# Order of transfers and of the key work in a three-part decoder kernel: the residual load goes ahead of the next x, and the preparation is rearranged

## The reference, cut to what matters

```
# 1. mixing: 8 heads of 64, fft along the head, running sum over the tokens
q, k, v = split(x @ w_qkv);  fq, fk, fv = fft(q), fft(k), fft(v)
kv = cumsum(fk * fv, over tokens)
x = layernorm(x + ifft(kv * conj(fq)).real @ w_out)
# 2. cross attention on the context: 16 heads of 32
q, k, v = x @ W_q + b_q, ctx @ W_k + b_k, ctx @ W_v + b_v
x = layernorm(x + softmax(mask(q k^T / sqrt(32))) v @ W_o + b_o)
# 3. feed-forward: kernel rounded to 4 bits, plus a low-rank term
scale = max(abs(kernel)) / 7;  w = clip(round(kernel / scale), -8, 7) * scale
x = layernorm(x + x @ w + bias + (x @ a) @ b)
```

## Time and profile before

| | us |
|---|---|
| median of 3 runs | 970.46 (970.12 to 971.36) |
| the profiled execution, its own time | 969.73 |
| its span | 967.9 |

### The profile page before, as it was taken

One profiled execution on the slowest core, in us unless ns is written; L12 is line 12 of the kernel. 1 busy time (PEld: TensorE's weight loads), 2 busy tenths in 40 slices (PEclk: granted clock), 3 DMA queues, 4 the chain that ended last, 5 costly groups with the idle time before them and its releaser, 6 DMA issues.

```text
span 967.9 us, 14663 instructions
## 1 busy us (share of the span) xinstructions
PE 895.2 (92%) x4344; PEld 737.5 (76%) x4344; DVE 683.1 (71%) x1152; ACT 377.2 (39%) x1414; POOL 346.8 (36%) x320
## 2 busy tenths in 40 slices
PE   7669999697979799999889999999999999999997
PEld 7448878586858587888678788888888888888775
DVE  3666666466557566755776787969879797887957
ACT  5413312010201101011186566565566565676610
POOL 0113556242405152435522431514334243441713
PEclk9799999799989899999999999999999999999999
DMA  9577365413132330304466532131222203120021
GB/s 265 141 254 179 127 194 193 131 44 103 72 87 87 87 126 5 131 11 170 140 249 202 165 90 70 29 128 24 78 73 73 80 22 110 42 89 19 17 76 44
DMA packets 107307, 102.19 MB, mean 106 GB/s; under 512 B 43287, under 2 KB 69143, under 8 KB 107263
## 3 DMA queue, kind: packets, MB, share of 16 engines
q1 hardware_dynamic: 107263, 101.64, 34.0%
HBM read 61.54 MB, written 40.08 MB: 105 GB/s over the span
## 4 chain that ended last, share of the span: by engine, by line
PE 42%; DMA 3%; DVE 2%; POOL 1%; issue 1%; ACT 1%; SPq 0%; POOLq 0%; DVEq 0%
PE shared_ps L62 32%; PE score_ps L62 4%; PE shared_ps L1379 4%; PE shared_ps L1342 1%; PE shared_ps L1412 1%; POOL probs L1760 1%; DMA values_split<-x_tok 1%; DMA w_o_and_ffn<-weights_split 1%; DMA x_tok<-residual_between 1%; DVE x_and_res L1948 0%; DVE xT_and_qT L1850 0%; ACT probs L1601 0%; POOL x_and_res L1769 0%; DVE y L1926 0%; POOL rstd L1753 0%
## 5 line engine op out<-in xcount | busy, mean ns | idle before, releaser
L1601 ACT ACTIVATE probs<-score_ps,top_s 128x77 f32<-128x77 f32 x512 | 158.9, 360 | 29.0 <-DVE top_s L1907 28.8
L1760 POOL TENSOR_TENSOR probs<-probs,per_total 128x616 f32<-128x616 f32 x64 | 83.2, 1316 | 116.4 <-DVE per_total L1914 116.2
L1601 ACT ACTIVATION_READ_ACCUMULATOR probs<-score_ps,top_s 128x1 f32 x512 | 124.1, 243 | 0.0
L62 PE MATMUL shared_ps<-w_o_and_ffn,xT_and_qT 128*128 128x512 f32 x384 | 96.7, 400 | 5.1 <-DVE xT_and_qT L1850 4.5
L62 PE MATMUL out_ps<-w_back_hi,xT_and_qT 128*128 128x512 f32 x224 | 76.3, 424 | 26.9 <-DVE mix_r L994 26.9
L1753 POOL TENSOR_TENSOR rstd<-ve,half_power 128x1 f32<-128x1 f32 x64 | 42.2, 659 | 163.6 <-DVE ve L1937 159.1
L62 PE MATMUL shared_ps<-w_o_and_ffn,xT_hi 128*128 128x512 f32 x256 | 88.2, 407 | 2.0 <-DVE xT_lo L1858 1.8
L62 PEld LDWEIGHTS shared_ps<-w_o_and_ffn,xT_and_qT 128*128 128x128 f32 x384 | 70.1, 188 | 22.2 <-DVE xT_and_qT L1850 4.1
L830 POOL TENSOR_TENSOR mix_rstd<-mix_ve,half_power 128x1 f32<-128x1 f32 x32 | 22.1, 690 | 162.9 <-DVE mix_ve L1002 162.9
L765 ACT ACTIVATE v_sb<-v_ps 128x512 f32<-128x512 f32 x32 | 18.4, 594 | 151.1 <-PE v_ps L62 151.1
L62 PEld LDWEIGHTS out_ps<-w_back_hi,xT_and_qT 128*128 128x128 f32 x224 | 45.1, 204 | 40.2 <-DVE mix_r L994 29.5
(11 more groups left out here) (193 smaller groups left out, 2301.4 us busy)
## 6 DMA issues: line engine op xcount, KB each, us to landing
x_tok<-in_x SPq DMA_DIRECT2D x32, 256.0 KB, 4.4
x_res<-in_x SPq DMA_DIRECT2D x8, 1024.0 KB, 7.2
x_between<-mix_x SPq DMA_DIRECT2D x32, 256.0 KB, 2.1
residual_between<-mix_res SPq DMA_DIRECT2D x32, 256.0 KB, 2.1
x<-x_between SPq DMA_DIRECT2D x8, 1024.0 KB, 5.5
x_tok<-residual_between SPq DMA_DIRECT2D x8, 1024.0 KB, 5.7
out<-y_out SPq DMA_DIRECT2D x32, 256.0 KB, 2.0
w_o_and_ffn<-weights_split SPq DMA_DIRECT2D x6, 1024.0 KB, 9.3
```

Of the source, the lines that this page charges most:

```text
L62: last = nc.tensor.matmul(out, l, r, start=(n == 0), stop=(n == len(terms) - 1))
L1601: nc.scalar.activation(probs[:, t % 2, j * KEYS:(j + 1) * KEYS], score_ps[:, g, k * KEYS:(k + 1) * KEYS], ACT.Exp, bias=top[:, t % 2, j:j ...
L1760: nc.gpsimd.tensor_tensor(p, p, per_total[:, t % 2, h * heads:(h + 1) * heads].unsqueeze(2) .to_broadcast([P, heads, KEYS]), ALU.mult).the ...
```

## The change

**In mixing** the loop of SP issues the residual load before the load of the next x. **In the preparation**

- the loads of w_out and of the inverse transform go ahead of those of the key bias, of `a` and `b`, and of x; `a` is loaded once instead of three times, and GpSimd copies it to the two other places;
- PE folds back 0 and 1 before it turns `a`; keys 0 to 2 come before, key 3 behind, the transpose of the maximum, and keys 4 to 7 behind the product a·b;
- the key bias is scaled once (`bias_kd`), and ScalarE applies bias and scale to each key block (`bias_keys`), from PSUM to `k_val`. PE waits for `k_biased` instead of `prod_used`;
- the splitting of W_k on VectorE comes before the turning of x, and two of the four turns of x come between key blocks;
- the maximum across rows is found by a transpose on PE and a reduction on VectorE;
- the context is stored as soon as it is turned, ahead of all key stores, and the feed-forward weight is stored last;
- the merges come one key block later, two and two.

```
--- before.py
+++ after.py
@@ SP, preparation
             sp.dma_start(raw_k[:], by_chunk(ins["W_k"])).then_inc(wk_loaded, 16)
+            sp.dma_start(wout_sb[:], by_chunk(ins["w_out"])).then_inc(out_loaded, 16)
+            sp.dma_start(inv[:], ins["dft_inverse"]).then_inc(out_loaded, 16)
             sp.dma_start(bias_k[:], ins["b_k"].rearrange("(c p) -> p c", p=P),
                          allow_slow_non_contiguous=True).then_inc(wk_loaded, 16)
-            load_blocks(sp, x_first, ins["x"][0], hand.x_loaded)
-
-            sp.dma_start(wout_sb[:], by_chunk(ins["w_out"])).then_inc(out_loaded, 16)
-            sp.dma_start(inv[:], ins["dft_inverse"]).then_inc(out_loaded, 16)
             sp.wait_ge(a_cleared, 1)
+            sp.dma_start(a_sb[:, :, 0:RANK], by_chunk(ins["a"])).then_inc(a_loaded, 16)
...
+            load_blocks(sp, x_first, ins["x"][0], hand.x_loaded)
...
+            sp.wait_ge(side_lo, len(SIDE))
+            for n, (at, size) in enumerate(tiles):
+                for part, tile in enumerate(ctxT):
+                    sp.dma_start(c_dram[n, part, :, :, 0:size], tile[:, :, at:at + size].bitcast(F32)).then_inc(ctx_stored, 16)
...
-                if n == NKEY - 3:
+                if n == NKEY - 1:
                     sp.wait_ge(merged_ready, NC)
                     sp.dma_start(by_chunk(ffn_dram), ffn).then_inc(ffn_stored, 16)
@@ PE, preparation
+                if m < 2:
+                    pe.wait_ge(prod_used, n - 1)
+                else:
+                    pe.wait_ge(k_biased, m - 1)
...
+            for m in range(3):
+                project_keys(m)
+            pe.wait_ge(top_ready, 1)
+            nc.tensor.transpose(turned[1][:, 0:P], top[:].to_broadcast([P, P]), ident[:]).then_inc(top_turned, 1)
+            project_keys(3)
@@ ACT, preparation
+            def bias_keys(m):
+                act.wait_ge(prod_ready, AT_KEY + m + 1)
+                if m >= 2:
+                    act.wait_ge(k_lo_ready, m - 1)
+                nc.scalar.activation(k_val[:, m % 2, :], prod[(AT_KEY + m) % 2][:, 0:half_rows], ACT.Identity,
+                                     bias=bias_kd[:, m // 2:m // 2 + 1], scale=float(XHD) ** -0.5).then_inc(k_biased, 1)
...
+            for m in range(NKEY):
+                bias_keys(m)
+                if 1 < m <= 1 + NC:
+                    x_copy(m - 2)
+                keys_hi(m)
@@ POOL, preparation
-            nc.gpsimd.partition_all_reduce(top_all[:], top[:], P, bass.bass_isa.ReduceOp.max).then_inc(top_spread, 1)
+            for k in (32, 64):
+                nc.gpsimd.tensor_copy(a_sb[:, :, k:k + RANK], a_sb[:, :, 0:RANK]).then_inc(a_copied, 1)
@@ DVE, preparation
-                nc.vector.tensor_scalar(k_val[:, m % 2, :], prod[n % 2][:, 0:half_rows], bias_k[:, m // 2:m // 2 + 1],
-                                        float(XHD) ** -0.5, ALU.add, ALU.mult).then_inc(k_biased, 1)
...
+            nc.vector.tensor_reduce(top_all[:], turned[1][:, 0:P], AX.X, ALU.max).then_inc(top_spread, 1)
@@ SP, mixing
-            def finish(i):
-                load_residual(i)
-                store(i)
...
             with sp.Fori(1, B - 3) as i:
+                load_residual(i)
                 load_x(i + 3)
-                finish(i)
+                store(i)
```

More of the change, by code:

```diff
@@ L268, in _, with fold_back @@
                 last.then_inc(prod_ready, 1)
[L269 to L275, removed]
+            def fold_back(f, free, count):
                 n = AT_BACK[f]
                 p, im = f // 2, f % 2
-                pe.wait_ge(prod_used, n - 1)
+                pe.wait_ge(free, count)
                 for h in range(2):
@@ L292, in _ @@
             pe.wait_ge(out_loaded, 32)
-            fold_back(0)
-            fold_back(1)
+            fold_back(0, prod_used, NFOLD - 1)
+            fold_back(1, prod_used, NFOLD)
+            pe.wait_ge(a_loaded, 16)
+            pe.wait_ge(a_copied, 2)
+            pe.wait_ge(wT_ready, NFOLD)
+            for c in range(NC):
+                last = nc.tensor.transpose(turned[0][0:LORA, c * P:(c + 1) * P], a_sb[:, c, :], ident[:])
+            last.then_inc(a_turned, 1)
             pe.wait_ge(side_lo, len(SIDE))
@@ L303, in _ @@
                 nc.tensor.matmul(side[c][:], aT[:, c * P:(c + 1) * P], b_both[:], start=True, stop=True).then_inc(low_ready, 1)
-            for m in range(2, NKEY):
+            for m in range(4, NKEY):
                 project_keys(m)
-            fold_back(2)
-            fold_back(3)
+            fold_back(2, k_biased, NKEY - 1)
+            fold_back(3, k_biased, NKEY)
         @block.scalar
@@ L340, in _ @@
             copy_folded(AT_BACK[1])
-            for c in range(NC):
-                act.wait_ge(x_turned, c + 1)
-                nc.scalar.activation(xT[0][:, c, :], x_turn[:, c, :], ACT.Copy).then_inc(x_hi, 1)
+            act.wait_ge(a_turned, 1)
+            nc.scalar.activation(aT, turned[0][0:LORA, :], ACT.Copy).then_inc(aT_ready, 1)
             act.wait_ge(b_loaded, 48)
@@ L346, in _, with keys_hi, x_copy @@
             nc.scalar.activation(b_both[:], b_raw[:], ACT.Copy).then_inc(b_ready, 1)
[L347 to L353, removed]
+            def bias_keys(m):
[4 more added lines that the diff above has]
+                                     bias=bias_kd[:, m // 2:m // 2 + 1], scale=float(XHD) ** -0.5).then_inc(k_biased, 1)
+            def keys_hi(m):
+                act.wait_ge(k_biased, m + 1)
+                wait_reuse(act, k_stored[m % SLOTS], 32 * (m // SLOTS))
+                nc.scalar.activation(out_hi[:, m % SLOTS, :], k_val[:, m % 2, :], ACT.Copy).then_inc(k_hi_ready, 1)
+            def x_copy(c):
+                act.wait_ge(x_turned, c + 1)
+                nc.scalar.activation(xT[0][:, c, :], x_turn[:, c, :], ACT.Copy).then_inc(x_hi, 1)
+            act.wait_ge(k_bias_scaled, 1)
+            for m in range(NKEY):
[3 more added lines that the diff above has]
+                keys_hi(m)
             copy_folded(AT_BACK[2])
@@ L361, in _ @@
             nc.gpsimd.memset(half_power[:], -0.5)
-            def x_remainder(c):
+            pool.wait_ge(a_loaded, 16)
+            for k in (32, 64):
+                nc.gpsimd.tensor_copy(a_sb[:, :, k:k + RANK], a_sb[:, :, 0:RANK]).then_inc(a_copied, 1)
+            for c in range(NC):
                 pool.wait_ge(x_hi, c + 1)
@@ L404, in split_wk, with turn_x @@
                                         ALU.subtract).then_inc(wk_lo_ready, 1)
+            def turn_x(c):
+                turn_block(nc, x_turn[:, c, :], x_first, c).then_inc(x_turned, 1)
+            dve.wait_ge(wk_loaded, 32)
+            for c in range(NC):
+                split_wk(c)
+            nc.vector.tensor_scalar(bias_kd[:], bias_k[:], float(XHD) ** -0.5, None, ALU.mult).then_inc(k_bias_scaled, 1)
+            split_folded(AT_BACK[0])
             dve.wait_ge(hand.x_loaded, 16 * P // BLOCK)
             dve.wait_ge(w_turned, NFOLD)
[L408 to L413, removed]
-            split_wk(3)
+            turn_x(0)
+            turn_x(1)
             split_folded(AT_BACK[1])
```

58 lines of the change are left out of this document (17 added, 41 removed).

## The result

The changed kernel takes 936.21 us in the median of 4 runs (930.93 to 937.93), the kernel before beside it 970.29 (969.11 to 971.36): ratio 0.964, 95% interval 0.960 to 0.968. The profiled execution took 935.72 us, its span is 933.8. The forecast was 933.8 us, with 927 to 943 as the range.

The account below looks back on a forecast made before the run. It took PE, 92% busy, as the bound, with gains only where PE stands still or a whole stage waits. Mixing 26.7 plus preparation 10.0 made 36.7 us, so 970.46 - 36.7 = 933.8 us, range 927 to 943.

Parts of the forecast that it names:

- steps 3 to 5: Mixing: with the residual load early, each becomes like Step 6, 20.7 us gained over the three.
- Step 6: Mixing step adding batch 5's residual, already loaded early as no x load stood ahead; the control, 45.63 us.
- Step 2: Mixing: earlier residual load and some clock given back gain 6.0 us, with 2.7 and 7.0 as the ends.
- then the 5.09 us go, and PE waits 3.1 us: Step 2: residual there at 172.5, so VectorE's load wait goes and PE waits 3.1 us instead of 8.2.
- About 0.9 us of clock given back: Step 2: PE's shorter wait returns about 0.9 us of clock, less than in step 3.
- Preparation: The stage ends 11.6 us earlier, less 1.6 for clock at the start of mixing: 10.0 us, from 5 to 14.
- I keep 36.3: Preparation: feed-forward weight load, issued at 30.57, lands 5.7 us later at 36.3, when its reduction can start.
- I cost this at nothing, and at 3 if the slow end holds: Preparation: key stores wait behind ten early context stores, key block 4 needing a slot; 0 us, or 3.
- I take 1.8, two hits: Preparation: GpSimd's subtractions of x collide with VectorE's key work, adding 1.8 us to the chain.
- Now it waits over 7 us: Start of mixing: PE stands still over 7 us after its folds, so slow matmuls cost 1.6 us, between 0 and 2.
- by the row it saves the 2.95 us wait: Preparation: taking the maximum across rows off GpSimd saves VectorE's 2.95 us wait, by the trace.
- The prediction's 4.6: Preparation: upper bound on collisions, if all 5.5 us of GpSimd's four subtractions stop VectorE.

Follow-up runs that it names:

- Experiment 9: Changed kernel with the residual load of batch 1 issued about 12 us earlier, out of the loop; 934.65 us, ratio 0.9626.
- experiment 5: Changed kernel with bias and scale of the keys back on VectorE; 936.66 us, ratio 0.9667.
- experiment 6: Changed kernel with four context stores early and two behind each of key blocks 0, 1 and 2; 932.65 us, ratio 0.9633.
- experiment 8: Changed kernel with four extra matmuls on PE behind the last fold, result unread; 933.7 us, ratio 0.9639.
- experiment 3: Changed kernel with the context stores put back, two behind each of key blocks 0 to 4; 935.61 us, ratio 0.9661.
- experiment 10: Changed kernel with GpSimd's four subtractions of x held back until the third rounding has ended; 933.83 us, ratio 0.9616.
- experiment 2: Changed kernel with the old order of SP's loop in mixing, so the preparation change alone; 960.23 us, ratio 0.990.
- experiment 1: Kernel before with only SP's loop order in mixing changed, residual load ahead of the next x; 941.15 us, ratio 0.9704.
- experiment 4: Changed kernel with the maximum across rows back on GpSimd, ahead of its subtractions of x; 936.55 us, ratio 0.9663.
- experiment 7: Changed kernel with the feed-forward weight stored in four parts, each behind its merge; 935.79 us, ratio 0.9657.
- experiment 11: Changed kernel with the edits of experiments 6, 7, 9 and 10 together; 932.12 us, ratio 0.9614.

## Why the prediction was right

The time was missed by 2.4 us, the total gain forecast as 36.7 and 34.1 measured.

**Mixing, steps 3 to 5: right as argued.** Step 6 was the experiment already made: 45.63 us a step forecast, 45.75 measured, in the whole change and in mixing alone (45.72).

**Step 2: right in kind, mis-sized.** The term "then the 5.09 us go, and PE waits 3.1 us": the load landed at 163.1, 1.1 us behind VectorE, and PE waited 4.13. "About 0.9 us of clock given back" did not come: PE's wait fell by 4.0 us and the step by 3.5, inside its stated ends. Experiment 9 puts the late landing at 0.8 us of PE's wait; the remaining 3.3 us are VectorE's own lateness, and in experiments 5 and 6, where the load was in time too, they are 3.0. The clock's part changes from one execution to the next: with the same wait experiment 8 has the 0.9 us. Step 2 took 48.2 to 51.9 us over the eleven traces with the new order. The forecast of 49.2 lies among them, and the kernel after happened to be traced near their upper end.

**Preparation: right in sum, by two errors that cancel.** "I keep 36.3" for the feed-forward weight was 2.8 us late: its load was issued at 26.11, not 30.57, and landed some 7.3 us later instead of 5.7. Which of the reordered transfers gave this, no run separates. "I cost this at nothing, and at 3 if the slow end holds" was wrong: the slot wait is 3.76 us on ScalarE, of which 1.70 reach VectorE (2.0 to 3.5 and at most 1.5 in the four other traces of this preparation), and experiments 3 and 6 take it away from block 4. "I take 1.8, two hits" was 3.3 us less the one of before, 2.4 (experiment 10), and some 1.4 in the traces of 2 and 8, which have one collision less. From the end of the reduction to the last merge it took 53.44 - 35.76 = 17.7 us, not 15.5, and from there to the next stage 4.9, not 5.3. So the stage ended 2.8 - 2.2 + 0.4 = 1.0 us ahead of the forecast. Against the kernel before, the same three pieces show where the 12.7 us come from: 8.2 because the reduction ends earlier (35.76, not 43.92), 0.3 from the chain to the last merge (17.95 before, 17.7 now), and 4.2 because the stage ends 4.9 us behind that merge and not 9.1. What was taken off VectorE and what came upon it, collisions and the slot wait included, nearly cancel.

**The start of mixing: right in size, wrong in cause.** "Now it waits over 7 us" made a longer standstill the reason. PE waited 5.08 us and lost 2.3; but experiment 1 lost 2.7 behind the 3.1 us of before. So the full clock of the earlier trace rows is what one execution of that preparation showed, and another of it did not; it is luck that the 1.6 us came near.

**The maximum.** The 2.95 us wait of before was real, but experiment 4 has GpSimd again and no wait: it went with the new order of VectorE, not with the transpose. Here too the prediction's "by the row it saves the 2.95 us wait" gives the edit a gain that the order had already brought. So the rule that speaks for GpSimd here (the Trainium skill, "GPSIMD Engine Reference", Engine selection) is neither helped nor hurt by the runs: both ways end within what a trace tells apart. On the collisions the runs go with the other (the Trainium skill, "SBUF — State Buffer", Who interferes with whom) in direction: all four instructions of VectorE that grew, by 0.38 to 1.08 us, lay beside GpSimd's, and without it none did. The prediction's 4.6 took every collision as VectorE's loss; the traces of 2 and 8 show that GpSimd can be the one that loses.

**What stays open.** What sets how long the clock stays at 1.2 GHz behind a like standstill. Executions of one kernel differ by 2 to 11 us; part of that is this clock, and how much is not shown. The medians of four to six runs can't confirm differences of 1 to 2 us that the traces show. And no experiment puts the old order of loads back, so that the 8.2 us of the earlier reduction come from it, and from the folding back that it lets go ahead, is read from the traces and not tested.

## What to carry to other kernels

Look in the trace for a repetition in which the disputed step is already absent (here the last batches, which had no x to load): its length is the forecast. A transfer that is wanted first and can be issued first belongs ahead in the queue; one that only fills a hole can hold up stores whose buffers someone waits for, as the context stores did here. Before a difference of 1 to 2 us between two traces is believed, look how far traces of the same code differ in that piece. When a wait disappears, take away the edit alone that was meant for it before crediting it, since a new order of the waiting engine may have hidden the wait anyway.

## What the runs showed of the hardware

- The time of one kernel goes with PE's mean granted clock only roughly: experiment 1 ran in 949.17 us at 0.979 and in 938.50 at 0.989, but experiment 8 in 935.63 at 0.991 and in 930.48 at 0.990.
- Behind a standstill of 3.1 to 3.2 us the next matmul of 512 columns took 0.47 us in one trace and 0.77 in two others. Behind waits of 3.0 to 4.3 us in step 2, matmuls ran at 1.2 GHz for 5 to 6 us in most traces, for about 3 in three of them (experiments 5, 6 and 8), and in experiment 11 not at all.
- An instruction of VectorE over 2048 columns took 2.32 us beside GpSimd's subtraction and 1.28 alone; a split of 308 columns up to 1.56 and 0.48. Where VectorE's began first (experiments 2 and 8), it took 1.27 and GpSimd's 2.20 and 2.23, for 1.29 in experiment 7.
- GpSimd's reduction across rows was done 6.3 us behind its input in the kernel before, and at most 3.9 us behind it in experiment 4. Two subtractions stood ahead of it before, but they ended at 44.15, 0.2 us behind the input at 43.92, so the difference stays open.
